# A fused transformer block: the opening in one block with eight banks, and the second attention's context made in the first three scan rounds

## What is computed

```python
x = x + L0_attn(layernorm(x), ...)      # a scan over the 16 batches: each step takes z = x@t_k.T,
                                        # y = x@t_v.T, one gradient step on a small MLP
                                        # (W1, b1, W2, b2), and puts x@t_q.T through the new MLP
x = x + L0_xattn(layernorm(x), ctx, mask_0)   # keys and values from layernorm(ctx)*g2 + b2
x = x + L0_ffn(layernorm(x))                  # 8 experts, top 2
x = x + L1_attn(layernorm(x))                 # 16 query heads, 8 key heads
x = x + L1_xattn(layernorm(x), ctx, ctx, mask_1)   # keys and values from ctx itself, k + bk
x = x + L1_ffn(layernorm(x))                  # 8 experts, top 2
```

## Time and profile before

| | us |
|---|---|
| median of 3 runs (709.66 to 713.04) | 710.86 |
| the profiled execution, own time | 711.03 |
| its span in the profile | 708.9 |
| TensorE / VectorE / ScalarE / GpSimd busy | 565.3 / 481.4 / 435.4 / 362.3 |
| chain that ended last: TensorE / GpSimd / issue / VectorE | 22% / 17% / 14% / 13% |
| mean granted clock of TensorE | 0.877 |

### The profile page before, as it was taken

One profiled execution on the slowest core, in us unless ns is written; L12 is line 12 of the kernel. 1 busy time (PEld: TensorE's weight loads), 2 busy tenths in 40 slices (PEclk: granted clock), 3 DMA queues, 4 the chain that ended last, 5 costly groups with the idle time before them and its releaser, 6 DMA issues.

```text
span 708.9 us, 18437 instructions
## 1 busy us (share of the span) xinstructions
PE 565.3 (80%) x6129; PEld 461.8 (65%) x6144; DVE 481.4 (68%) x1350; ACT 435.4 (61%) x913; POOL 362.3 (51%) x646
## 2 busy tenths in 40 slices
PE   3796999998997715999849999996987873399990
PEld 1485778776775615999735776764665652299990
DVE  6653468888687452555458999985899986155554
ACT  1453278886684323888526767665786852388872
POOL 5711434665488573566535434321454867355661
PEclk9997569998798756999959999999899997599995
DMA  7749980000000012222190000000000001122216
GB/s 199 223 152 336 337 281 1 2 3 2 9 16 25 24 41 54 77 70 72 38 366 22 2 2 2 2 2 1 2 3 10 25 24 41 51 75 72 72 44 189
DMA packets 42169, 52.66 MB, mean 74 GB/s; under 512 B 11277, under 2 KB 37213, under 8 KB 41789
## 3 DMA queue, kind: packets, MB, share of 16 engines
q1 hardware_dynamic: 33277, 40.04, 18.0%
q0 software_dynamic: 4544, 9.35, 4.0%
q10 hardware_dynamic: 4256, 2.10, 1.0%
HBM read 41.04 MB, written 28.22 MB: 98 GB/s over the span
## 4 chain that ended last, share of the span: by engine, by line
PE 22%; POOL 17%; issue 14%; DVE 13%; DMA 3%; ACT 2%; SPq 0%; POOLq 0%; ACTq 0%; DVEq 0%
POOL yo L1592 10%; PE p_pT L1432 6%; PE p_s L1418 3%; PE p_o L1458 3%; POOL xs L1131 3%; PE p_o L1463 3%; DVE x_prob L1177 3%; DVE x_inv L1184 2%; POOL to_row L1587 2%; DVE x_top L1167 2%; PE p_s L1409 2%; DMA back<-yo 1%; PE p_s L1700 1%; ACT x_pT L1325 1%; DMA xs<-send,x_index 1%
## 5 line engine op out<-in xcount | busy, mean ns | idle before, releaser
L1592 POOL DMA_INDIRECT yo<-context,to_row x78 | 76.0, 975 | 65.6 <-POOL to_row L1587 51.4
L1654 ACT ACTIVATE context<-pack 128x1156 f32 x78 | 90.6, 1166 | 26.5 <-DVE context L1626 17.6
L1700 PE MATMUL p_s<-xT_f,context 128*128 128x128 f32 x624 | 85.8, 282 | 0.0
L1700 PEld LDWEIGHTS p_s<-xT_f,context 128*128 128x128 f32 x624 | 79.3, 199 | 0.0
L1131 POOL DMA_INDIRECT xs<-send,x_index x64 | 64.1, 1001 | 22.1 <-issue 15.9
L1619 DVE TENSOR_SCALAR context<-p_s,context 128x128 f32<-128x128 f32 x156 | 47.5, 346 | 34.1 <-PE p_s L1700 34.1
L1325 ACT ACTIVATE x_pT<-p_pT 128x512 f32<-128x512 f32 (+1 forms) x96 | 48.8, 524 | 28.4 <-PE p_pT L1432 26.1
L1661 ACT ACTIVATE context<-p_s,context 128x128 f32<-128x128 f32 x156 | 47.6, 355 | 21.6 <-PE p_s L1700 12.0
L1432 PE MATMUL p_pT<-sq,x_prob 128*128 128x128 f32 x320 | 54.4, 297 | 6.3 <-ACT x_pT L1325 5.5
L1167 DVE TENSOR_REDUCE x_top<-p_s 128x12 f32<-128x924 f32 (+2 forms) x48 | 46.9, 1006 | 15.9 <-PE p_s L1418 15.8
L1177 DVE TENSOR_TENSOR x_prob<-p_s,x_top 128x768 f32<-128x768 f32 (+2 forms) x96 | 50.0, 576 | 0.1
(11 more groups left out here) (257 smaller groups left out, 1498.6 us busy)
## 6 DMA issues: line engine op xcount, KB each, us to landing
xs<-in_blank SPq DMA_DIRECT2D x2, 8707.5 KB, 42.8
pack<-in_pack SPq DMA_DIRECT2D x16, 578.0 KB, 9.2
context<-xs SPq DMA_DIRECT2D x78, 64.5 KB, 1.8
back<-yo SPq DMA_DIRECT2D x6, 256.0 KB, 4.7
back<-yo ACTq DMA_DIRECT2D x6, 256.0 KB, 5.6
yo<-context,to_row POOLq DMA_INDIRECT x78, 2.3
x<-in_x SPq DMA_DIRECT2D x4, 256.0 KB, 4.4
xs<-send,x_index POOLq DMA_INDIRECT x64, 2.4
```

What stands on the lines that cost most here:

```text
L1592: nc.gpsimd.indirect_dma_start(yo[:, :], bass.IndirectOffsetOnAxis(to_row[:, n % NY, :], 0), y[:, n % NY, :], None).then_inc(y_stored[n % ...
L1654: nc.scalar.activation(ws[:, n % NW, :], pack[:, bass.ds(e, 1), :].rearrange("p a w -> p (a w)"), ACT.Copy).then_inc(ws_ready, 1)
L1700: ins = mm(p_h[n % 2][k // 2][:, P * (k % 2):P * (k % 2 + 1)], ws[:, n % NW, P * k:P * (k + 1)], xT[:, n % 2, :], start=True, stop=True)
```

## The change

- The two blocks of prelude become one, with all eight banks in use (two for p_x, two for p_q). In the x part the turn of group g + 1 stands behind q^T of group g, e0^T waits for tkv alone (the cast of the identity moves behind the first context group), and context normalisation alternates with the adds, group by group.
- prelude makes the context of the first attention only. ScalarE spreads both parts. The last keys are spread from key 61 on, 16 wide, so that no zeroed gap is needed, and the second attention's probabilities stand at the end of each strip. The raw keys of context 1 are loaded into ctx_k[1], behind the weights.
- New `second_context`: four groups of the second context in the tables of the scan rounds. ScalarE spreads the keys into pT and prob of the first attention (rounds -1, 0, 1, 1), TensorE makes values and k in p_s banks 0, 1, 2 (groups 0 and 1 behind g2 in rounds 0 and 1, group 2 behind "a" in round 2, group 3 behind g2 in round 2), VectorE writes the masked values and adds bk to k (at the end of rounds 0 and 1, behind w2n in round 2, at the end of round 2). Scores of batch 0 wait until all of it is read; so does the copy of the first turned probabilities for the last values.
- Setup of hT, hqT, h moves from the main block into prelude's GpSimd; mask copies and blank rows move from prelude's second block to the head of SyncE's main block.

```diff
 FIRST_PE = ((3, "score"), (0, "aT"), (1, "aq"), (0, "a"),
+    ({2: 2}, "c1_third"), (4, "tp0"), (5, "po"), (0, "eT"), ...
-    (2, "project"), (0, "g2"), (0, "g1"), ...
+    (2, "project"), (0, "g2"), ({0: 0, 1: 1, 3: 2}, "c1"), (0, "g1"), ...
 FIRST_DVE = (..., (0, "eTa"), (5, "res"), (1, "w2n"),
+    ({2: 2}, "c1_third"), (0, "slope2"), ...
+    (0, "b1n"), (0, "w2Tn"), ({0: 0, 1: 1, 3: 2}, "c1"))
 FIRST_ACT = (..., (3, "exp"), (7, "c_rlg"),
+    ({0: -1, 1: 0, 2: 1, 3: 1}, "c1"))
...
+            p_x = [ps(f"p_x{u}", pctx) for u in range(2)]
+            p_zT, p_qT, p_e0T, p_z = (ps(f"p_{n}", pctx) for n in ("zT", "qT", "e0T", "z"))
+            p_q = [ps(f"p_q{u}", pctx) for u in range(2)]
+            p_k, p_v, p_r = p_zT, [p_qT, p_e0T], [p_z, p_q[0]]
...
+                    for g in groups:
+                        count(dve, *of_c, g)
+                        if g:
+                            norm_c(g - 1)
+                        dve.wait_ge(q_ready, g + 1)
+                        nc.vector.tensor_tensor(flat(x, g), p_q[g % 2][:, :], flat(x, g), ALU.add).then_inc(q_added, 1)
+                    norm_c(groups[-1])
...
+                    turn_c(0)
+                    for g in groups:
+                        if g + 1 < len(groups):
+                            turn_c(g + 1)
+                        pe.wait_ge(cT_sb, g + 1)
...
+                        wait(pe, k_sb, g)
+                        mm(p_k[:, 0:GC], m["w"]("x0_k"), flat(cnT, g), start=True, stop=True).then_inc(k_ready, 1)
+                        wait(pe, v_kept, 2 * (g - 1))
+                        pe.wait_ge(c_spread, 2 * (g + 1))
+                        values(p_v[g % 2], p_r[g % 2], mm, firsts[:, g % 2], lasts[:, g % 2], m["w"]("x0_v")).then_inc(v_ready, 1)
...
+def second_context(nc, m):
+    GS, s = 4, m["c1"]
+    p_v, p_r, p_k = (m["p_s"][:, n, :] for n in range(3))
+    keysT = m["ctx_k"][1]
...
+        def products(g, u):
+            wait(pe, s["read"], 3 * g)
+            pe.wait_ge(s["spread"], 2 * (g + 1))
+            values(p_v, p_r, mm, m["spread"][u][:, 0], m["spread"][u][:, 1], m["w"]("x1_v")).then_inc(s["v"], 1)
+            mm(p_k[:, 0:GS * TC], m["w"]("x1_k"), flat(g), start=True, stop=True).then_inc(s["k"], 1)
...
+        def copies(g, u):
+            if g == 0:
+                act.wait_ge(m["loaded_rest"], 16 * m["n_rest"])
+            wait(act, s["v"], g - 1)
+            for to, keys in spread(m["spread"][u][:, 0], m["spread"][u][:, 1], keysT, g):
+                nc.scalar.activation(to, keys, ACT.Copy).then_inc(s["spread"], 1)
...
+        def keep(g, u):
+            dve.wait_ge(s["v"], g + 1)
+            keep_values(nc, m, 1, g, p_v, p_r, s["read"])
+            dve.wait_ge(s["k"], g + 1)
+            nc.vector.tensor_scalar(flat(g), p_k[:, 0:GS * TC], m["col"]("x1_bk"), None, ALU.add).then_inc(s["read"], 1)
...
+def values(p_v, p_r, mm, first, last, wv):
+    for j in range(4):
+        of = slice(P * j, P * (j + 1))
+        mm(p_v[:, of], first[:, j, :], wv, start=True, stop=True)
+        ins = mm(p_r[:, of], last[:, j, :], wv, start=True, stop=True)
+    return ins
...
             if FIRST + b == 0 and mask:
                 pe.wait_ge(m["masks_placed"], 64 * NG)
+                pe.wait_ge(m["c1"]["read"], 3 * (NB // 4))
```

More of the change, by code:

```diff
@@ L54, in returned @@
     return [range(end - n, end) for n, end in zip(RETURN[q], ends)]
-CONTEXT_LOADS = 6
+CONTEXT_LOADS = 4
 SCAN_LOADS = 5
@@ L233, in build @@
         m["countdown"] = sb("countdown", [P, NE])
+        m["mk_0"] = sb("mk_0", [NB, TC], BF16)
+        m["mk_1"] = sb("mk_1", [NB, 3, TC], BF16)
+        room_v = sb("room_v", [P, 2 * NH * STRIP])
+        m["v_s1"] = carve(room_v)(2, NH, STRIP)
+        m["scan_work"] = scan_work(carve(room_v))
+        m["scan_sems"] = {n: sem("t_" + n) for n in SCAN_SEMS}
+        m["masks_made"] = sem("masks_made")
+        m["c1"] = {n: sem("c1_" + n) for n in ("k", "v", "read", "spread")}
         loaded_scan = sem("loaded_scan")
@@ L315, in _ @@
                 f0["gpsimd"](pool)
+                pool.wait_ge(m["c1"]["read"], 3 * (NB // 4))
                 staggered(s1["gpsimd"](pool) + later(x1["gpsimd"](pool)))
@@ L330, in _ @@
             def _(act):
-                staggered(rotation(FIRST_ACT, {**ts["scalar"](act), **x0["scalar"](act)}))
+                staggered(rotation(FIRST_ACT, {**ts["scalar"](act), **x0["scalar"](act), "c1": c1["scalar"](act)}))
                 f0["scalar"](act)
@@ L405, in prelude @@
             cnT = csb("cnT", [P, NB, TC])
-            ctxT = csb("ctxT", [P, NB, TC])
-            first = csb("first", [P, 3, GS, P])
-            last = csb("last", [P, 3, GS, P])
+            firsts, lasts = csb("firsts", [P, 2, GS, P]), csb("lasts", [P, 2, GS, P])
             mk_u8 = pctx.enter_context(nc.sbuf_tensor("mk_u8", [NB, TC], U8))
@@ new lines, in spread @@
+def spread(first, last, keysT, g):
+    GS = 4
+    keys = keysT[:, GS * g:GS * (g + 1), :]
+    for to, at, n in ((first, 0, KM), (last, TC - KR, KR)):
+        yield (to.rearrange("p b (r k) -> p b r k", k=n), keys[:, :, at:at + n].unsqueeze(2).to_broadcast([P, GS, P // n, n]))
+def values(p_v, p_r, mm, first, last, wv):
[4 more added lines that the diff above has]
+    return ins
@@ new lines, in keep_values @@
+def keep_values(nc, m, q, g, p_v, p_r, done):
+    GS = 4
+    strips = m["ctx_v"][q][:, GS * g:GS * (g + 1), :].rearrange("k b (n r d) -> k (b n) r d", r=4, d=2 * DH)
+    nc.vector.tensor_tensor(strips[:, :, 0:4:3, :], p_v[:, :].rearrange("k (n r d) -> k n r d", r=2, d=2 * DH),
+                            m["keep_v"][:, :].unsqueeze(1).unsqueeze(1).to_broadcast([P, GS * NG, 2, 2 * DH]),
+                            ALU.mult).then_inc(done, 1)
+    nc.vector.tensor_tensor(m["ctx_vr"][q][:, GS * g:GS * (g + 1), :].rearrange("k b (n d) -> k (b n) d", d=8 * DH),
+                            p_r[:, :].rearrange("k (n d) -> k n d", d=8 * DH),
+                            m["keep_vr"][:, :].unsqueeze(1).to_broadcast([P, 2 * GS, 8 * DH]), ALU.mult).then_inc(done, 1)
@@ L1323, in run @@
                     wait(act, mixed, FIRST + b)
+                    if beside and b == 0:
+                        act.wait_ge(m["c1"]["v"], NB // 4)
                     of = slice(sets[g][0], sets[g][-1] + 1)
```

491 lines of the change are left out of this document (218 added, 273 removed).

## The result

| | us |
|---|---|
| changed kernel, median of 20 runs (696.94 to 705.74) | 700.07 |
| kernel before beside it, median of 20 runs (704.47 to 713.48) | 710.13 |
| ratio, 95% interval | 0.9884 [0.9857, 0.991] |
| the profiled execution, own time / span | 701.3 / 699.5 |
| TensorE / VectorE / ScalarE / GpSimd busy | 560.5 / 479.0 / 438.3 / 358.9 |

The change makes the kernel 10 us faster; 697.2 was forecast, with a range of 691.5 to 705. TensorE's busy time fell by 4.8 us; the rest of the gain is waiting time. The single times of one kernel can fall into two groups (13 of the changed kernel's 20 lie from 696.9 to 701.3 us, 7 from 703.8 to 705.7; e11's six lie at 689.0 to 690.9 and 696.4 to 698.2), only one execution of each kernel was profiled, and no run shows what divides the groups.

What follows compares the result with a forecast made beforehand. Waits bound the x part, TensorE's work the contexts, a loop through all engines the rounds. From 711.0: opening -18.0, hand-over to a^T -1.7, rounds 0 to 2 +10.0, rounds 3 and 4 -4.1, giving 697.2 us; range 691.5 to 705.

Steps and rivals of the forecast that it cites:

- one of the prediction's own signs of being wrong: Granted clock 0.50 in rounds 3 and 4 was listed as showing the prediction wrong.
- The x part and the context, -18.0: Opening: x part and first attention's context end at 42.3 us against 60.32, so 18.0 us less.
- Rival (b): Opening bound by hand-overs, not TensorE: groups at 3.7 instead of 2.7 us, total 701.5; chance 0.12.
- Block end to first a^T, 1.1 us: Opening's end to first scan matmul: 1.1 us instead of 2.81, GpSimd's setup being done, so -1.7.
- SyncE's transfers at nothing: Mask copies and blanking transfers issued some 4 us later, wanted later still, so no cost.
- The lock: Opening: VectorE's cast waits up to 3.6 us for GpSimd's memset on shared ports; total grows by 0.6 us at most.
- Rounds 0 to 2, 31.9 us: First three scan rounds, now holding the second context: 31.9 us instead of 21.85, so +10.0.
- Rounds 3 and 4, 16.0 us: These scan rounds run at full clock, 16.0 us instead of 20.09, so -4.1.
- Rival (a): Clock level falls in the wait before the first scores; rounds 3 and 4 stay at 20.1, total 701.3; chance 0.16.
- the one row of an idle stretch: Profile before: 60 to 63 us without a matmul, granted 1.00, followed by 0.50; cited as evidence about the clock's fall.
- After round 4, nothing: Later rounds: same instructions but for a few waits long since met, so no change in time.
- the likeliest case: The forecast itself, 697.2 us with rounds 3 and 4 at full clock; chance 0.52.

Runs made afterwards that it cites:

- e11: Changed kernel with second context's first group ahead of round 0, the others one round earlier, and ten unread products in TensorE's waits: 693.63 us, 0.9763.
- e6: Changed kernel with the identity's cast back ahead of the first e0 products and the first ctx_v memset back beside it: 711.21 us, 0.9916.
- e12: Changed kernel with only the identity's cast back ahead of the first e0 products, the memset left where the change put it: 701.34 us, 0.9895.
- e0: Changed kernel again, no edit, as yardstick on another chip: 708.44 us, 0.9895 of the kernel before.
- e2: Changed kernel without the second context (values zero, keys raw), of use for its time alone: 697.48 us, 0.9738.
- e9: Changed kernel a third time, no edit, as yardstick on a third chip: 700.73 us, 0.9881 of the kernel before.
- e3: Changed kernel with two unread 512-column products in TensorE's wait ahead of the first scores: 705.46 us, 0.9858.
- e10: Changed kernel with nine unread products in TensorE's waits, from the opening's end to the scores of round 4: 691.80 us, 0.9754.
- e7: Changed kernel with the whole second context ahead of round 0 and seven unread products in TensorE's waits: 706.78 us, 0.9833.
- e1: Changed kernel with all four groups of the second context ahead of round 0, in two sets of three banks: 708.89 us, 0.9900.
- e5: Changed kernel with the second context's first group ahead of round 0 and the other three one round earlier: 706.31 us, 0.9844.
- e4: Changed kernel with seven unread products in TensorE's waits, from the opening's end to the first scores: 703.32 us, 0.9807.

## Why the prediction was right, point by point

The time lies in the range because the opening came out as worked out, and the opening is the larger part. One term of the sum, rounds 3 and 4, did not come in, and with it one of the prediction's own signs of being wrong was there, a granted clock of 0.50 in these rounds. The term for rounds 0 to 2 was 2.1 us too small for this profile.

- **The x part and the context, -18.0.** Right, at -18.6. Last write at 41.7 us for 42.3; a group of the x part takes 3.89 us for 3.9, and once x is there TensorE waits for no more than 0.7 us at a time. Rival (b), hand-overs, did not occur. Some 9.6 us of it are work that only moved, into the rounds. Of the rest, e6 and e12 show what the order of cast and memset is worth; the double banks and the single block were not tried by themselves.
- **Block end to first a^T, 1.1 us.** 1.11.
- **SyncE's transfers at nothing.** Right as far as the first scores show: they wait for VectorE, not for the masks.
- **The lock.** Right as a mechanism and harmless where the change put it. The cast took 1.99 us beside the memset of the second ctx_v, in the changed kernel's timeline:

```profile
32.38 3.52 POOL L514 MEMSET context<- 128x4096 f32 x1
...
32.79 0.69 DVE L718 TENSOR_TENSOR context<-p_qT,keep_v 128x512 f32<-128x512 f32 x1 [2.62 <-PE p_z L710]
...
34.00 1.99 DVE L550 CAST ident_bf<-sq 128x128 bf16<-128x128 f32 x1
```

  The products of group 3 did not wait for it. The masked copy beside the same memset keeps its 0.69 us. It reads PSUM and the cast does not; whether that is the reason, no run shows.
- **Rounds 0 to 2, 31.9 us.** 34.0 in the first profile, 31.6 and 31.5 in the other two. Round by round, for forecasts of 10.1, 6.85 and 14.95: 10.5, 6.6 and 14.5 in e0, and 10.7, 8.0 and 15.2 in the first, whose rounds 1 and 2 were not at 1.00 throughout. The 10.1 is 3.8 us over the 6.34 of before; no run shows that term by itself, but beside e2's round 0 of 6.3 us the one with the first group took 4.1 to 4.4 us more. The queue that the working drew for round 2 (group 2, its read, eT, group 3, its read, scores) is what the timeline shows, up to the release of the scores by the read of k.
- **Rounds 3 and 4, 16.0 us: the term that was mis-sized.** 20.8 in the first profile, 20.2 in the other two. Rival (a) happened in all three: the level falls 0.3 us before (first) or 1.0 us after (e0, e9) the end of the 2.27 us wait before the first scores. The working had the wait (2.7 us, "with next to nothing") and set the products just before it against the one row of an idle stretch. The row was right; dense work just before a wait did not protect the level. e3 and e10 show it by filling the waits.
- **After round 4, nothing.** Half right: the instructions were the same, the clock was not. The changed kernel's rounds 5 to 14 took 94.5 us against 96.2, which gave back 1.8 of the 4.8 us; in its repetitions they took 96.7 and 96.3.

In numbers, for the profiled execution: opening to first a^T -20.3 (forecast -19.7), rounds 0 to 2 +12.1 (+10.0), rounds 3 and 4 +0.7 (-4.1), rounds 5 to 14 -1.8 (0); with the rest -0.2, the span is 9.5 us shorter, against 13.8. So the sign and the range held by the opening; the likeliest case was not the one that happened, and the 700.07 of the median lies by rival (a)'s 701.3. That it lies so near is in part luck: against rival (a)'s terms the opening was 0.6 us shorter, rounds 0 to 2 were 2.1 and rounds 3 and 4 0.7 us longer, and rounds 5 to 14 1.8 us shorter by a dip of the clock that took another form.

**What stays open.** Not every fall has a wait. In e10 and e12 the level fell at 141.6 and 141.2 us, where TensorE was busy without a gap over 0.4 us; and e11 lost it in a place where e10, with the same waits and products, kept it. In the first profile it fell at 56.5 us with no wait over 0.3 us in that round. And a longer wait than e3's or e7's can pass without a fall, e10:

```profile
42.61 0.38 PE L880 MATMUL p_s<-back,scan_w1T 128*32 128x128 f32 x2 [1.57 <-PEq L658]
```

So waits of 0.9 to 2.4 us are where the level was lost for long in rounds 0 to 4, but their length is no law of when. Rounds 11 to 14 come in two forms: with a round 12 of 14.9 to 15.0 us (before, e0, e1, e2, e3, e5, e9, e11) or of 11.1 to 12.9 (changed, e4, e6, e7, e10, e12), 1.5 to 4.2 us apart in the sum of rounds 11 to 14. In the first, TensorE waits in round 12 for VectorE's add, and the level is low for 13.7 us after it; e9:

```profile
159.10 0.46 PE L931 MATMUL p_o<-scan_w2T,room_v 128*128 128x128 f32 x2 [2.02 <-DVE x L1209]
```

e4 has the same wait of 2.02 us, and there the level was low for 6.8 us in two pieces. What decides between the two was not tried, and no product was put into that wait. Medians that differ by less than 4 us can owe it to this.

## What to carry to other kernels

Price a wait of the matrix engine at its own length plus what the next stretch costs at the lower level: 2.3 us of waiting here cost 2.9 us more in the two rounds behind it (20.16 against 17.22), and nine products of about 1 us each whose result nobody reads, put into waits, brought the kernel from 700.7 to 691.8 us, of which 5.4 us lie in the rounds where they stand. When a profile blames a small VectorE instruction of an odd length, look for the GpSimd instruction that covers it before moving the small one. And work moved into a loop hides only in idle time that is there: the second context cost 9.8 us inside the rounds, for about 9.6 us of products at full clock.

## What the runs showed of the hardware

- From 71.8 to 88.6 us TensorE was busy 16.05 of 16.8 us in e9, and the granted clock stood at 0.50 all the time. In e10 the same rounds (71.1 to 88.3) ran at 1.00, with no wait over 0.90 us.
- The level fell in or within 1.0 us of short waits of TensorE: 2.27 us (changed, e9), 1.10 us (e3), 1.00 us (e7). With the first of them filled, in e3, e4 and e10, it did not fall there. A wait of 1.57 us in e10 was followed by no fall.
- A memset of 4096 columns (3.51 us) holds up normalising tiles and casts in SBUF for its whole length (6.39 for 2.93 us, 3.41 for 0.21), and leaves a masked copy out of PSUM, run wholly beside it, at 0.69.
- The table load of ScalarE took 1.28 us in each profile and stood in front of hT in round 0; in e4 and e10 two of the added products stood in TensorE's wait for it.
